# Unrolling attention's groups into one order, loading the first group during the projection, and moving the routing steps into attention

## The chip, the cores and the metric

The kernel runs on one core of a Trainium2 chip. Its time is the device time of one execution in microseconds (us). It was run three times: 2694.41, 2698.81 and 2700.54 us, with a median of 2698.81 us. The engines are named as in the profile: PE (TensorE), PEld (its weight loads), DVE (VectorE), ACT (ScalarE), POOL (GpSimd), and SP (SyncE), which only starts transfers here.

## What is computed

Two layers. Each one normalises its input, runs an attention and a routed feed-forward part on it, and adds the product of the two to the input. The change touches the first layer's attention and the routing of its feed-forward part:

```python
xn = _layernorm(x, axis=-1)                      # x: [2, 2048, 256]
# attention: 16 heads of 16 channels, causal, exact softmax
q, k, v = (xn @ W.T).reshape(B, S, 16, 16).transpose(0, 2, 1, 3)   # for Wq, Wk, Wv
p = softmax(where(mask, q @ k.T / 4, min)); out = (p @ v) @ Wo.T
# routing: 8 experts, each takes its first C = 4096/8 = 512 tokens
logits = x_flat @ router_w; probs = softmax(logits)
expert_idx = argmax(probs); gate = probs[expert_idx]
pos = cumsum(onehot)[expert_idx] - 1; keep = pos < C
expert_in.at[expert_idx, clip(pos, 0, C - 1)].add(x_flat * keep)
...
x = x + attention * silu(feed_forward)
```

## The kernel before, in words

The program is a row of stages, each a block that all engines enter and leave together: constants, projection (`stage_project`), attention (`stage_attention`), experts, a join, and the second layer. The change touches projection and attention.

**Projection.** 4096 tokens go through in 8 chunks of 512 (`NC`), four for each of the two sequences. For each chunk DVE normalises, PE turns the rows and multiplies them, and ACT and DVE together split each of q and k into three bf16 parts (`parts`, four tiles m = 0 to 3, each with parts 0, 1, 2). ACT makes the first part (`first`), DVE the rest (`rest_of`), ACT the second part, DVE the third. SP then stores them to `qk_parts` and v to `v`. `parts` is one buffer, so ACT's `first(m)` of a chunk waits until the store of the chunk before has landed (`parts_stored[m]`). POOL keeps a copy of the normalised rows (`xn_all`). After the last chunk DVE computes the routing from `logits` in 22 small steps (the first maximum, its one-hot form, counts through two matmuls of PE, the place of each token, the gate), with one exponential on ACT.

**Attention.** A group is four heads of one sequence; there are 8 groups (g), even ones of sequence 0, odd ones of sequence 1, and `u = g % 2` picks the buffers `qa`, `kb` (the parts of q and k, stacked to 96 rows) and `vg` (v with a column of ones). Each group needs three kinds of work:

- A steps: PE multiplies 128 queries by up to 512 keys into one of three `ring` banks, DVE takes the row maxima of it (`a_best`, line 859). There are 160 in a group: 16, 32, 48 and 64 for the query chunks c = 0 to 3.
- M and MT: after a chunk's last A step DVE negates the maxima and splits them in three (M), PE turns them and DVE copies them out (MT), and SP stores them as three further rows of `qa` (`store_rows`).
- S, PV, COPY, O: with those rows in place PE computes the scores again transposed (S, `a_pss`, line 774), ACT takes the exponential (line 836), PE multiplies by v (PV, `a_acc`, line 792), ACT copies the sums (COPY), PE turns them (O) and DVE divides.

An S step of chunk c waits for the chunk's three rows (`m_landed[c]`). `attention_steps` writes the order out by hand: a head of A steps up to half of group 0's cost (`LEAD = 0.5`), and then for each group a list in which its S and PV steps are woven with the second half of its own A steps and the first half of the next group's. Each group's list ends with its own last PV, COPY and O. All engines follow it in order: three times round a hardware loop over two groups (`groups`), then the last two groups written out. SP loads the next group (24 transfers of q, 6 of k, 4 of v) when a group begins. The first group is loaded after the projection has ended: q and v by SP (`load_q`, `load_v`), k by ACT.

POOL meanwhile sets `vg` and the ones in `kb`, writes zeros over `expert_in` (16 transfers) and then scatters the rows of `xn_all` to their experts' slots (32 indirect transfers).

Of the kernel before, what the change touches and what calls it, by code (L numbers as in the profile page):

```python
# [24 lines left out]
P = 128  # L25
# [194 lines left out]
def stage_project(nc, io, keep, dram):  # L220


    with ExitStack() as ctx:
# [14 lines left out]
        parts = st.sb("parts", [P, 4, 3, CH], BF16)  # L238
        vout = st.sb("vout", [P, 2, TC, D])
        spare = st.sb("spare", [P, 1])  # L240
        logits = st.sb("logits", [P, E, NT])
        top = st.sb("top", [P, NT])
        equal = st.sb("equal", [P, E, NT])
        first = st.sb("first", [P, NT])
        onehot = st.sb("onehot", [P, E, NT])
        onehot16 = st.sb("onehot16", [P, E, NT], BF16)
        shifted = st.sb("shifted", [P, E, NT])
        expd = st.sb("expd", [P, E, NT])
        total = st.sb("total", [P, E, NT])
        scanned = st.sb("scanned", [P, E, NT])  # L250
        place = st.sb("place", [P, E, NT])
        small = st.sb("small", [P, 6, NT])
# [12 lines left out]
        parts_stored = [st.sem(f"parts_stored{k}") for k in range(4)]  # L265
# [3 lines left out]
        onehot_ready, counted, shifted_ready, exp_ready = (st.sem("onehot_ready"), st.sem("counted"),  # L269
                                                           st.sem("shifted_ready"), st.sem("exp_ready"))  # L270
# [3 lines left out]
        @block.gpsimd  # L274
        def _(pool):
            def keep_copy(c, n, u):

                pool.wait_ge(xn_ready, c + 1)
                pool.tensor_copy(keep["xn_all"][:, bass.ds(c * TC, TC), :], xn[:, u, :, :]).then_inc(xn_kept, 1)

            chunks_skewed(pool, keep_copy, lambda c, n, u: None)

        @block.sync
        def _(sp):
# [18 lines left out]
            def store(c, u):  # L303
                at = snap(sp, c * CH)
                for m in range(4):
                    rows = dram["qk_parts"][m // 2, :, (m % 2) * P:(m % 2 + 1) * P, bass.ds(at, CH)]
                    sp.wait_ge(parts_ready, 4 * c + m + 1)
                    sp.dma_start(rows.rearrange("r p n -> p r n"), parts[:, m, :, :]).then_inc(parts_stored[m], 16)
# [13 lines left out]
            for m in range(4):  # L322
                sp.wait_ge(parts_stored[m], 16 * NC)
            for u in range(2):
                sp.wait_ge(v_stored[u], 16 * (NC // 2))

        @block.vector
        def _(vec):
# [34 lines left out]
            def back(c, n, u):  # L363
                def rest_of(m):

                    vec.wait_ge(first_part, 4 * c + m + 1)
                    vec.scalar_tensor_tensor(out=rest[:, m, :], in0=psq[m][:, :], scalar=HD ** -0.5 if m < 2 else 1.0,
                                             in1=parts[:, m, 0, :], op0=ALU.mult, op1=ALU.subtract).then_inc(rest_ready, 1)

                def third(m):  # L370
                    vec.wait_ge(second_part, 4 * c + m + 1)
                    vec.tensor_tensor(parts[:, m, 2, :], rest[:, m, :], parts[:, m, 1, :], ALU.subtract
# [4 lines left out]
                for m in range(4):  # L377
# [5 lines left out]
            ch.base, ch.k = NORM_STEPS * NC, 0  # L383


            vec.wait_ge(v_copied, NT)
            L = logits[:, :, :]
            first_max(vec, ch, keep, L, top[:, :], equal[:, :, :], first[:, :], onehot[:, :, :])
            vec.tensor_copy(onehot16[:, :, :], onehot[:, :, :]).then_inc(onehot_ready, 1)
            vec.tensor_tensor(shifted[:, :, :], L, top[:, :].unsqueeze(1).to_broadcast([P, E, NT]), ALU.subtract  # L390
                              ).then_inc(shifted_ready, 1)
            vec.wait_ge(exp_ready, 1)
            den, kept, chosen, clipped, slot = (small[:, k, :] for k in range(5))
            ch.link(vec.tensor_reduce(den, expd[:, :, :].rearrange("p e t -> p t e"), X, ALU.add))
            ch.link(vec.reciprocal(keep["gate"][:, :], den))
            vec.wait_ge(counted, 1)
            places(vec, ch, keep, "running0", psq[0][:, 0:E * NT], psq[1][:, 0:E * NT], total[:, :, :], scanned[:, :, :],
                   place[:, :, :])
            ch.link(vec.tensor_tensor(place[:, :, :], place[:, :, :], onehot[:, :, :], ALU.mult))
            ch.link(vec.tensor_reduce(chosen, place[:, :, :].rearrange("p e t -> p t e"), X, ALU.add))  # L400
            ch.link(vec.tensor_scalar(kept, chosen, float(CAP0), None, ALU.is_lt))
            ch.link(vec.tensor_tensor(keep["gate"][:, :], keep["gate"][:, :], kept, ALU.mult))
            ch.link(vec.tensor_scalar(clipped, chosen, float(CAP0 - 1), None, ALU.min))
            ch.link(vec.scalar_tensor_tensor(out=slot, in0=first[:, :], scalar=float(CAP0), in1=clipped,
                                             op0=ALU.mult, op1=ALU.add))
            ch.link(vec.tensor_copy(keep["slot_get"][:, :], slot))

            ch.link(vec.scalar_tensor_tensor(out=clipped, in0=kept, scalar=-SKIP, in1=slot, op0=ALU.mult, op1=ALU.add))
# [83 lines left out]

def attention_steps():

    maxima, ends = [], []
    for c in range(QC):
# [1497 lines left out]
```

## Time and profile before

| What | us |
|---|---|
| median of 3 runs | 2698.81 (2694.41 to 2700.54) |
| span of the profiled execution | 2692.8 |
| PE busy in the span | 2451.3 (91%) |
| DVE busy | 1846.2 (69%) |
| ACT busy | 1406.8 (52%) |
| POOL busy | 815.1 (30%) |
| v_rows<-p_vout, issue to landing, median | 5.1 |
| a_qa<-a_neg_rows in the attention, issue to landing: least, median, most | 1.6, 1.9, 3.5 |
| last transfer of attention issued by ACT | 1156.86 |

The span runs from the first to the last instruction of one profiled execution; the measured time also holds what lies before and after. The profiled execution's own measured time is not given apart; the median of the runs is 6.0 us above its span. The mean granted PE clock over the span is 0.953 of full speed. Times in rows are counted from the span's start, so an instruction's place in the table of stages can be read off directly: projection until about 133, attention from there to about 1159.

### The profile page before, as it was taken

The page shows a single profiled execution, that of the slowest core. Times are in us where ns is not written, and L with a number is a line of the kernel's source. Part 1 is how long each engine was busy: PE and PEld are TensorE (multiplying, and loading weights), DVE is VectorE, ACT ScalarE, POOL GpSimd, SP SyncE. Part 2 cuts the span into 40 slices and gives each one's busy share as a digit, 9 for nine tenths or more (in the row PEclk, how much of TensorE's full clock was granted, in tenths as well). Part 3 has the DMA queues.
Part 4 walks back from the last instruction along what each step waited for, and adds up shares of the span by engine and source line. Part 5 has one row for each costly group of instructions (what it writes and reads, how often), then busy time and mean ns, then how long its engine had stood idle before and what let it go on. Part 6 is the DMA issues. An engine that isn't in the chain of part 4 may idle for free. (4 is left out here: it accounts for less than half of the span.)

```text
span 2692.8 us, 51134 instructions
## 1 busy us (share of the span) xinstructions
PE 2451.3 (91%) x16420; PEld 1589.0 (59%) x16420; DVE 1846.2 (69%) x3682; ACT 1406.8 (52%) x2776; POOL 815.1 (30%) x647
## 2 busy tenths in 40 slices
PE   5648999999999999969977599999999999999999
PEld 4512333333333333358866477777777777777777
DVE  7757877877787777424438476777667767766776
ACT  3404655656565566755634255555555555555554
POOL 1070000000000000014425355554455555444553
PEclk9858999999999999989988699999999999999999
DMA  4574041321404040033257000000000000000000
GB/s 135 191 170 65 5 62 26 41 52 16 61 6 62 6 60 5 7 127 133 102 177 241 18 13 12 11 13 13 13 13 13 9 11 13 13 13 13 13 9 9
DMA packets 189865, 132.85 MB, mean 49 GB/s; under 512 B 99857, under 2 KB 177687, under 8 KB 189712
## 3 DMA queue, kind: packets, MB, share of 16 engines
q1 hardware_dynamic: 160048, 100.06, 15.4%
q10 hardware_dynamic: 24160, 14.16, 2.2%
q0 software_dynamic: 5504, 16.69, 1.7%
q8 instruction: 83, 1.36, 0.2%
q14 instruction: 70, 0.57, 0.1%
HBM read 84.43 MB, written 46.14 MB: 48 GB/s over the span
## 5 line engine op out<-in xcount | busy, mean ns | idle before, releaser
L859 DVE TENSOR_REDUCE a_best<-a_ring 128x1 f32<-128x512 f32 (+3 forms) x1280 | 700.9, 604 | 214.0 <-PE a_ring L721 123.0
L836 ACT ACTIVATE a_probs<-a_pss 128x1024 f32<-128x1024 f32 (+3 forms) x640 | 554.0, 895 | 452.6 <-PE a_pss L777 228.7
L721 PE MATMUL a_ring<-a_kb,a_qa 96*128 96x512 bf16 (+3 forms) x1280 | 453.0, 365 | 67.2 <-DVE a_best L859 32.3
L774 PE MATMUL a_pss<-a_qa,a_kb 99*128 99x512 bf16 (+3 forms) x1280 | 433.9, 353 | 15.6 <-issue 7.2
L1771 ACT ACTIVATE w_probs<-w_pss,w_top 128x256 f32<-128x256 f32 x512 | 239.0, 476 | 379.7 <-DVE w_top L1859 365.0
L1606 POOL TENSOR_TENSOR w_probs<-w_probs,w_inv 128x512 f32<-128x512 f32 x256 | 301.0, 1176 | 395.7 <-DVE w_inv L1865 386.3
L962 POOL TENSOR_TENSOR e_w_r<-e_w,e_w_r 128x1024 fp32r<-128x1024 f32 x28 | 67.0, 2402 | 1032.7 <-ACT e_w_r L1035 1032.7
L1629 PE MATMUL w_psw<-wqkv,w_xr 128*128 128x512 f32 x1152 | 301.5, 398 | 11.6 <-POOL w_xr L1563 11.6
L774 PEld LDWEIGHTS a_pss<-a_qa,a_kb 99*128 99x128 bf16 x1280 | 123.5, 98 | 302.6 <-ACT a_probs L836 224.5
L792 PE MATMUL a_acc<-a_probs,a_vg 128*32 128x512 f32 (+3 forms) x2560 | 299.9, 541 | 0.1
L1669 PE MATMUL w_pss<-w_kd,w_qt 128*128 128x256 f32 x1536 | 278.4, 310 | 0.0
L1859 DVE TENSOR_REDUCE w_top<-w_pss 128x2 f32<-128x512 f32 x256 | 176.8, 691 | 141.5 <-PE w_pss L1669 140.7
L721 PEld LDWEIGHTS a_ring<-a_kb,a_qa 96*128 96x128 bf16 x1280 | 126.4, 99 | 223.9 <-DVE a_best L859 128.6
L1629 PEld LDWEIGHTS w_psw<-wqkv,w_xr 128*128 128x128 f32 x1152 | 205.6, 190 | 47.6 <-POOL w_xr L1563 12.1
L1669 PEld LDWEIGHTS w_pss<-w_kd,w_qt 128*128 128x128 f32 x1536 | 222.0, 195 | 4.1
L1629 PE MATMUL w_psw<-we,w_xr 128*128 128x512 f32 x768 | 204.2, 401 | 0.0
L1710 PE MATMUL w_pso<-w_pt,w_v 128*64 128x128 f32 x2048 | 168.3, 285 | 0.1
L1689 PE MATMUL w_pst<-identity,w_probs 128*128 128x128 f32 x1024 | 155.7, 275 | 0.0
L1629 PEld LDWEIGHTS w_psw<-we,w_xr 128*128 128x128 f32 x768 | 134.9, 188 | 22.9 <-issue 0.2
L1689 PEld LDWEIGHTS w_pst<-identity,w_probs 128*128 128x128 f32 x1024 | 123.6, 140 | 31.2 <-issue 5.7
L1882 DVE SCALAR_TENSOR_TENSOR w_y<-w_psw,coef,w_y 128x256 f32<-128x256 f32 x224 | 108.3, 484 | 42.4 <-PE w_psw L1629 23.2
L1710 PEld LDWEIGHTS w_pso<-w_pt,w_v 128*64 128x64 f32 x2048 | 106.5, 136 | 49.6 <-issue 49.1
(223 smaller groups left out, 3771.2 us busy)
## 6 DMA issues: line engine op xcount, KB each, us to landing
e_w<-in_w SPq DMA_DIRECT2D x16, 1024.0 KB, 7.9
qk_parts<-p_parts SPq DMA_DIRECT2D x32, 384.0 KB, 3.7
a_qa<-qk_parts SPq DMA_DIRECT2D x192, 64.0 KB, 2.5
a_kb<-qk_parts SPq DMA_DIRECT2D x42, 256.0 KB, 9.5
p_xin<-in_x SPq DMA_DIRECT2D x8, 512.0 KB, 5.4
v_rows<-p_vout SPq DMA_DIRECT2D x8, 512.0 KB, 5.1
a_vg<-v_rows SPq DMA_DIRECT2D x32, 128.0 KB, 9.1
expert_in<-zero POOLq DMA_DIRECT2D x16, 256.0 KB, 8.3
```

Source lines behind the costliest of these rows:

```text
L721: ins = pe.matmul(bank[:, 0:keys], qa[u][0:QR, i // TC, h, (i % TC) * P:(i % TC + 1) * P], kb[u][0:QR, h, k * CH:k * CH + keys], start=Tru ...
L774: ins = pe.matmul(pss[idx % 2][:, e, lo:CH], kb[u][0:MR, h, j * P:(j + 1) * P], qa[u][0:MR, c, h, lo:CH], start=True, stop=(j < TC * c))
L792: ins = pe.matmul(acc[32 * h:32 * h + 32, lo:CH], vg[u][:, j, h, :], probs[:, 2 * (pv % 2) + h // 2, h % 2, lo:CH], start=(j == 0), stop=( ...
L836: act.activation(probs[:, idx % 4, :, lo:CH], pss[idx % 2][:, :, lo:CH], ACT.Exp).then_inc(exp_done, 1)
L859: vec.tensor_reduce(best[:, i // TC, h * TC + i % TC, k:k + 1], bank[:, 0:keys], X, ALU.max).then_inc(ring_taken, 1)
L1606: pool.tensor_tensor(probs[:, p % 4, :, :], probs[:, p % 4, :, :], inv[:, :, p:p + 1].to_broadcast([P, 2, 2 * P]), ALU.mult).then_inc(p_re ...
L1629: ins = pe.matmul(psw[bank][:, :], xr[a][:, src, k, :], moving(b, k), start=(m == 0), stop=(m == len(pairs) - 1))
L1669: ins = pe.matmul(scores, qt[a][:, p, :], keys[b][:, p, :, :], start=False, stop=(a, b) == PARTS[-1])
L1689: ins = pe.transpose(pst[r % 2][:, 2 * e + role, :], probs[:, p % 4, e, role * P:(role + 1) * P], keep["identity"][:, :])
L1710: ins = pe.matmul(pso[e * DH:(e + 1) * DH, p % 4, :], v[(u + 1 + role) % 2][:, h * DH:(h + 1) * DH], pt[:, p % 2, 2 * e + role, :], start= ...
L1771: ins = act.activation(probs[:, p % 4, e, :], pss[p % 2][:, e, :], ACT.Exp, bias=top[:, e, p:p + 1], accum_out=rows[:, e, p:p + 1])
L1859: vec.tensor_reduce(top[:, :, p], pss[p % 2][:, :, :], X, ALU.max, negate=True).then_inc(top_ready, 1)
```

## The change

There are four parts.

1. `attention_plan` replaces `attention_steps`. It makes one order for all 8 groups; no engine has a loop in the attention any more. A steps lead the S steps by 0.3 of a group at first (`LEAD0`), then grow at 1.3 times the rate of S (`RAISE`) up to a lead of 0.6 (`LEAD`). So the head has 53 A steps in place of 84, group 1's A steps begin at 0.54 of group 0's S work, and the last 0.6 of the last group has no A step. A group's last O now stands some steps into the next group.
2. The first group's q, k and v are loaded by POOL in the projection, after its copy of chunk 5 (`c == NC // B + 1`), once chunks 0 to 3 are stored. The buffers of even groups and `logits` live in `EarlyGroup`. POOL sets the ones and zeros in them when the projection starts.
3. `parts` has two buffers, one for each parity of the chunk.
4. The routing steps stand in the attention's order, one (`RT`) behind each of the first 22 A steps of group 2, that is from 1.40 to 1.51 groups of S work. The scatter waits for the last of them (`slots_ready`).

The core of the diff:

```diff
@@ projection, POOL
-            chunks_skewed(pool, keep_copy, lambda c, n, u: None)
+            ch.link(pool.memset(early.vg[:, :, :, :], 0.0))
+            ch.link(pool.memset(early.vg[:, :, :, HD:HD + 1], 1.0))
+            ch.link(pool.memset(early.kb[QR:MR, :, :], 1.0))
+            for c in range(NC):
                 pool.wait_ge(xn_ready, c + 1)
+                pool.tensor_copy(keep["xn_all"][:, c * TC:(c + 1) * TC, :], xn[:, c % 2, :, :]).then_inc(xn_kept, 1)
+                if c == NC // B + 1:
+
+                    for u in range(2):
+                        for m in range(4):
+                            pool.wait_ge(parts_stored[u][m], 16 * NC // B // 2)
+                        pool.wait_ge(v_stored[u], 16 * NC // B // 2)
+                    group_k(pool, dram, [early.kb], 0, early.k_landed)
+                    group_q(pool, dram, [early.qa], 0, early.q_landed)
+                    group_v(pool, dram, [early.vg], 0, early.v_landed)
@@ projection, ACT
-                    wait(act, parts_stored[m], 16 * c)
-                    act.activation(parts[:, m, 0, :], psq[m][:, :], ACT.Copy, scale=HD ** -0.5 if m < 2 else 1.0
+                    wait(act, parts_stored[u][m], 16 * n)
+                    act.activation(parts[:, u, m, 0, :], psq[m][:, :], ACT.Copy, scale=HD ** -0.5 if m < 2 else 1.0
@@ the order
-LEAD = 0.5
+LEAD0, LEAD, RAISE = 0.3, 0.6, 1.3
+ROUTE_STEPS = 22
+ROUTE_AT = 2
+    def wanted(done):
+
+        at = done / total
+        return LEAD0 + RAISE * at if RAISE * at + LEAD0 < at + LEAD else at + LEAD
+
+    def advance(done, turn_later):
+        nonlocal found, routed
+        while found < wanted(done) * whole:
+            u = next(ahead, None)
+            if u is None:
+                return
+            if u[0] == "MT" and turn_later:
+                late.append([u, 6])
+                continue
+            steps.append(u)
+            if u[0] == "A":
+                found += cost(u[2:])
+                if u[1] >= ROUTE_AT and routed < ROUTE_STEPS:
+                    steps.append(("RT", routed))
+                    routed += 1
@@ attention, SP
+            begun = -1
+            for s, r in plan:
+                if s[0] == "S" and s[1] > begun:
+                    begun = s[1]
+                    if begun + 1 < GROUPS:
+
+                        wait(sp, pv_done, begun * n_pv)
+                        load(begun + 1)
                 if s[0] == "MT":
-                    store_rows(0, s[2], r)
+                    assert s[1] <= begun + 1
+                    store_rows(s[1], s[2], r)
@@ attention, POOL
             pool.wait_ge(cleared, 16 * n)
+            pool.wait_ge(slots_ready, 1)
```

On POOL the order of instructions in the projection shows where the first group's transfers stand. `p_` names are the projection's, `g_` those of the early group, `a_` the attention's:

```order
-L274 UNCONDITIONAL_BRANCH
-L279 COPY xn_all<-p_xn 128x1024 x3
+L261 UNCONDITIONAL_BRANCH
+L264 MEMSET g_vg 128x2048
+L266 MEMSET g_vg 128x64
+L267 MEMSET g_kb 3x8192
+L270 COPY xn_all<-p_xn 128x1024 x6
+L562 DMA g_kb<-qk_parts 16x4x2048 x6
+L553 DMA g_qa<-qk_parts 16x4x512 x24
+L571 DMA g_vg<-v_rows 128x16x16 x4
+L270 COPY xn_all<-p_xn 128x1024 x2
```

The three sets and 34 transfers are new there; two copies of rows stand behind the transfers.

On PE, before, the end of the head and the first S step (line 774) stand behind the A steps (line 721, with its mask on line 724) of chunk 2, and behind a loop's entry:

```order
L721 MATMUL a_ring<-a_kb,a_qa 128x512 x2
L721 MATMUL a_ring<-a_kb,a_qa 128x384
L724 MATMUL a_ring<-mask_qk,identity 128x128
L721 MATMUL a_ring<-a_kb,a_qa 128x512 x3
L724 MATMUL a_ring<-mask_qk,identity 128x128
L632 UNCONDITIONAL_BRANCH
L632 ISA
L773 ISA
L774 MATMUL a_pss<-a_qa,a_kb 128x512
```

After, on PE, the same place: the turn of chunk 1's maxima (line 729), five A steps of chunk 2, and the first S step (line 755):

```order
L729 MATMUL a_ring<-identity,a_neg_parts 128x128
L702 MATMUL a_ring<-g_kb,g_qa 128x512 x2
L702 MATMUL a_ring<-g_kb,g_qa 128x128
L705 MATMUL a_ring<-mask_qk,identity 128x128
L702 MATMUL a_ring<-g_kb,g_qa 128x512 x2
L755 MATMUL a_pss<-g_qa,g_kb 128x512
L758 MATMUL a_pss<-mask_kq,identity 128x128
```

So 31 A steps of group 0 moved behind the first S step, and the branches are gone.

On DVE, after, the routing steps stand between the maxima (line 904) of group 2's first A steps:

```order
L904 TENSOR_REDUCE a_best<-a_ring 128x1
L845 TENSOR_REDUCE a_top<-g_logits 128x32
L904 TENSOR_REDUCE a_best<-a_ring 128x1
L847 TENSOR_TENSOR a_r_equal<-g_logits,a_top 128x256
L904 TENSOR_REDUCE a_best<-a_ring 128x1
L849 SCALAR_TENSOR_TENSOR a_r_equal<-a_r_equal,expert 128x256
L904 TENSOR_REDUCE a_best<-a_ring 128x1
L852 TENSOR_REDUCE a_first<-a_r_equal 128x32
```

Before, they stood behind the projection's last `p_parts` and ahead of everything in the attention.

## Rows read from the trace of the kernel before

**Rows 1.** Busy time of each engine by stage (windows); x is a count.

```profile
core 0: us, PE busy (x) PEld busy (x) DVE busy (x) ACT busy (x) POOL busy (x), PEclk, DMA share, GB/s
78.00:122.00 44.00, 34.23 (x195) 29.09 (x193) 32.86 (x89) 26.72 (x68) 2.09 (x2) 0.96 0.57 192
133.00:151.00 18.00, 0.00 (x0) 0.00 (x0) 0.00 (x0) 0.00 (x0) 17.77 (x7) 0.50 1.01 126
183.00:215.00 32.00, 6.73 (x17) 1.30 (x16) 6.71 (x12) 0.00 (x0) 21.01 (x22) 0.50 0.30 111
...
340.60:458.70 118.10, 113.08 (x788) 43.23 (x788) 93.33 (x192) 71.09 (x85) 0.00 (x0) 1.00 0.25 37
...
1058.80:1160.00 101.20, 94.32 (x662) 32.46 (x662) 48.51 (x98) 70.37 (x85) 0.00 (x0) 1.00 0.04 8
```

**Rows 2.** Timeline at the projection's end: start, us, engine, line [idle before <-releaser].

```profile
113.03 0.60 ACT L425 ACTIVATE p_parts<-p_psq 128x512 bf16<-128x512 f32 x1 [1.93 <-DMA qk_parts<-p_parts]
122.88 0.58 DVE L144 TENSOR_REDUCE p_top<-p_logits 128x32 f32<-128x256 f32 x1
123.97 1.10 SPq L310 DMA_DIRECT2D v_rows<-p_vout  x1
132.09 0.18 DVE L409 TENSOR_SCALAR slot_put<-p_small 128x32 uint32<-128x32 f32 x1
```

**Rows 3.** Timeline of the first group's load and the first A step.

```profile
144.22 24.40 SPq L683 DMA_DIRECT2D a_vg<-v_rows  x4
151.23 0.29 PE L721 MATMUL a_ring<-a_kb,a_qa 96*128 96x128 bf16 x1 [24.79 <-DMA a_kb<-qk_parts]
```

**Rows 4.** Timeline of the head, up to the first S step.

```profile
161.28 16.03 DVE L859 TENSOR_REDUCE a_best<-a_ring 128x1 f32<-128x512 f32 x32 [0.21 <-PE a_ring L721]
178.86 0.22 DVE L876 COPY a_neg_rows<-a_ring 48x128 bf16<-48x128 bf16 x1 [0.38 <-PE a_ring L731]
182.57 38.85 SPq L641 DMA_DIRECT2D a_qa<-qk_parts  x24
203.69 0.29 DVE L859 TENSOR_REDUCE a_best<-a_ring 128x1 f32<-128x128 f32 x1 [4.90 <-remote]
223.60 0.63 PE L774 MATMUL a_pss<-a_qa,a_kb 99*128 99x512 bf16 x1
```

**Rows 5.** Waits in 223:1160: who waited for whom, us, times, longest.

```profile
PE a_pss L774 <- issue: 7.2, 2, 3.6
PE a_ring L802 <- ACT a_sums L844: 6.1, 8, 0.8
PE a_pss L774 <- DMA a_qa<-a_neg_rows: 5.8, 4, 1.6
```

**Rows 6.** Issue of transfers on SP and POOL: timeline, and the tile expert_in.

```profile
72.57 1.05 POOL L279 COPY xn_all<-p_xn 128x1024 f32 x1 [10.70 <-DVE p_xn L216]
75.68 2.75 SPq L308 DMA_DIRECT2D qk_parts<-p_parts  x4
...
L668 POOL DMA_INDIRECT expert_in<-xn_all,slot_put x32: 977/982/1042, 169.5 to 209.4; - x32
L665 POOL DMA_DIRECT2D expert_in<-zero x16: 539/542/771, 150.8 to 159.0; - x16
...
355.21 14.25 SPq L683 DMA_DIRECT2D a_vg<-v_rows  x4
1205.90 0.84 POOL L986 DMA_DIRECT2D expert_out<-e_yout  x1 [5.19 <-DVE e_yout L1093]
```

**Rows 7.** Timeline rows in which POOL and DVE use SBUF.

```profile
12.27 0.17 DVE L212 COPY p_var<-p_mv 128x4 f32<-128x4 f32 x1
16.30 1.43 POOL L279 COPY xn_all<-p_xn 128x1024 f32<-128x1024 f32 x1 [10.54 <-DVE p_xn L216]
137.02 13.79 POOL L660 MEMSET a_kb<- 3x8192 bf16 x2
```

**Rows 8.** Timeline of ACT near the attention's end.

```profile
1145.93 4.02 ACT L836 ACTIVATE a_probs<-a_pss 128x1024 f32<-128x1024 f32 x4 [0.26 <-PE a_pss L774]
```

More of the change, by code:

```diff
@@ L382, in _ @@
             chunks_skewed(vec, front, back)
[L383 to L408, printed above, removed]
-            ch.link(vec.tensor_scalar(keep["slot_put"][:, :], clipped, SKIP, None, ALU.add))
         @block.scalar
@@ L519, in attention_steps @@
     whole = sum(cost(u) for u in maxima)
-    lead, at = 0, 0
-    while at < LEAD * whole:
-        at += cost(maxima[lead])
-        lead += 1
-    def flow(lo, hi, dg):
-        for n in range(lo, hi):
-            yield ("A", dg, *maxima[n])
+    pairs = [(g, c, j) for g in range(GROUPS) for c in range(QC) for j in range(TC * (c + 1))]
+    total = sum(width(c, j) for g, c, j in pairs if g == 0) * GH
+    ahead = []
+    for g in range(GROUPS):
+        for n, u in enumerate(maxima):
+            ahead.append(("A", g, *u))
@@ L568, in attention_steps @@
[L568 to L588 removed]
+                ahead += [("M", g, c), ("MT", g, c)]
@@ new lines, in attention_plan @@
+    ahead = iter(ahead)
+    steps, late, found, routed = [], [], 0, 0
+    def wanted(done):
[16 more added lines that the diff above has]
+                    routed += 1
@@ new lines, in attention_plan @@
+    done = 0
+    advance(0, False)
+    for n, (g, c, j) in enumerate(pairs):
+        for h in range(GH):
+            steps.append(("S", g, c, j, h))
+            done += width(c, j)
+            advance(done, True)
+            for item in late:
+                item[1] -= 1
+            while late and late[0][1] <= 0:
+                steps.append(late.pop(0)[0])
+        if n:
+            pg, pc, pj = pairs[n - 1]
+            steps.append(("PV", pg, pc, pj))
+            if pj == TC * (pc + 1) - 1:
+                steps.append(("COPY", pg, pc))
+                late.append([("O", pg, pc), 6])
@@ L849, in _ @@
+            store(*turned_at[1:])
         @block.vector
@@ L872, in take_rows @@
-            def take_rows(c, r, bank, landed):
-                vec.wait_ge(ring_full, r + 1)
-                wait(vec, m_landed[(c - 2) % QC], landed)
-                vec.tensor_copy(neg_rows[:, c % 2, :], bank[0:3 * GH * TC, 0:P // 2].bitcast(BF16)).then_inc(ring_taken, 1)
+            L, (equal, onehot, shifted, expd, scanned, place) = logits[:, :, :], (big[n][:, :, :] for n in big)
+            before, total = counts[:, 0, :, :], counts[:, 1, :, :]
+            den, kept, chosen, clipped, slot = (small[:, k, :] for k in range(5))
```

565 lines of the change are left out of this document (281 added, 284 removed).

## The prediction, made before the changed kernel was run

> **What bounds the kernel now.** I read the table of stages first, then the timeline across the two stages that change, then the waits of the attention. The stages show two kinds of time [rows 1]. In the stream of the attention PE bounds: in the whole group from 340.6 to 458.7 PE is busy 113.1 of 118.1 us, DVE 93.3, ACT 71.1. Work that moves into this stream costs PE time; work that leaves other engines there costs nothing. Ahead of the stream nearly nothing is bound by PE: from 133 to 151 PE and DVE do nothing at all, and from 183 to 215 both work under 7 of 32 us.
>
> The timeline gives the reasons. The projection ends with 9.4 us of routing on DVE, 122.88 to 132.27 [rows 2]. Then the first group is loaded, and PE's first A step at 151.23 has waited 24.8 us for `a_kb` [rows 3]. The head runs at DVE's pace, 32 maxima in 16.03 us, and has finished chunks 0 and 1 at 179.1; then it stalls: at 203.69 DVE takes a tile that PE multiplied about 10 us before. That stretch begins when SP starts the next group's q transfers (182.57; 24 of them take 38.85 us) while POOL's scatter runs (169.5 to 209.4), and ends soon after the scatter. The first S step is at 223.60 [rows 4]. In the stream the chain of waits holds little: 7.2 us in two places where PE goes round the loop, 6.1 us before the O of each group, 5.8 us for the maxima's rows at chunk 3 [rows 5].
>
> **The sum, part by part.** It is made against the profiled execution (span 2692.8; the median is 6.0 us above it, and I carry this over).
>
> *Start of the attention.* Routing leaves the end of the projection, but the block can't end before the last v store has landed: issued at 123.97, with the 5 us that such a store takes, 129 [rows 2]. The second `parts` buffer draws that in. In the middle of the projection DVE bounds and nothing is gained. In the last two chunks, which have no normalisation beside them, ACT waits for the stores before (1.93 us at 113.03, about as much a chunk earlier, and DVE and PE wait behind it [rows 2]): 4.6 us. So the store lands at 124.3, and the next stage's first instruction follows 0.6 us later, as now. For contention and for the start (below) I add 2.4 us, between 0 and 9: first A step at 127.3, not 151.2. **-23.9 us.**
>
> This rests on the load being hidden. POOL is free after its copy of chunk 5 (72.57), chunk 3 is stored about 83.3 (its stores begin at 75.68, and v's comes last) [rows 6]. The 30 transfers of q and k have 64 rows each; the zeros' transfers, 128 rows, take 0.54 us: 16.2 us. v's 4 transfers have 2048 pieces of 64 bytes. No row shows such a transfer on POOL: below it lies 0.54, above it the scatter's pace, 1.29 us for 128 rows, or 20.6 us. `expert_out` (512 rows, 0.84 us) in proportion gives 3.4, and SP takes 3.6 for the same transfer [rows 6]; I take 3.4. POOL is then done at 83.3 + 16.2 + 13.6 = 113.1, with its last two copies at 115.2, 9 us before the store lands. If each v transfer took over 5.6 us, the stage would end later by the surplus. The bytes fit: the DMA queues are at 0.57 from 78 to 122 [rows 1].
>
> One new cost is at the start. POOL now sets `g_kb` from about 8.3 for 6.9 us, while DVE's first small copies start at 12.27 [rows 7]. If the two exclude each other, the projection starts up to 3.0 us later. They can get in each other's way: POOL's copy of rows takes 1.43 us at 16.30 beside a DVE cast, and 1.05 later [rows 6, 7]. This trace agrees there with the Trainium skill, SBUF — State Buffer, section Who interferes with whom: an operation of DVE in its two-port modes and one of GpSimd hold a shared port for the whole instruction.
>
> *Head.* Now 72.4 us, 151.2 to 223.6. Chunks 0 and 1 stay (27.6 us [rows 3, 4]), then 5 A steps instead of 36 at 0.5 to 0.55 us: 30.4 us. The stall between 183 and 215 has no place here: SP's load of group 1 starts when S begins, and the scatter has moved away from it. **-42.0 us.** First S step at 157.7.
>
> *Stream, now 223.6 to 1157.3.* Two trips round the loop go: **-7.2**. Seven of eight group ends no longer drain before O (0.78 us each): **-5.5**. The wait for the maxima's rows goes in steady groups, where M of chunk 3 now leads by 0.17 of a group, -5.8 and a little more that PEld shows; but in group 0 the lead is thin. Chunk 2's maxima turn 2.5 full-width S steps ahead of need and chunk 3's 1.5, or 2.4 and 1.4 us, against 6 us from turn to landing: about +8 for both, the first just behind SP's v transfers. Together **+0.3**, with -6 and +6 as bounds.
>
> The 31 A steps that left the head are now PE's work. The last group, with 76 A steps in place of 160, lasts 98.5 us where a whole one lasts 118.4 [rows 1]: 0.26 us per step missing, with little of the wide ones' difference in it, so **+8.1**. Routing costs 9.4 us of DVE [rows 2] at 1.40 to 1.51 of the stream, a stretch of 12 us. There the A steps are of chunk 0, short for PE, and DVE alone needs about 12 us for them and their M. PE is only three banks ahead, so little of it hides: between 0 and 9.4, I take **+7**. From 0 to 1.0 the A steps run at 1.3 times the pace; DVE (93.3 x 1.3 = 121 us) then comes close to PE's 130: **+3** (0 to 8). In the last 0.6 group there are no A steps; full-width exponentials go back to back at 1.005 us [rows 8], 2.0 a pair of tiles against PE's 1.92, for some 20 pairs: **+2** (0 to 4).
>
> Sum: -23.9 - 42.0 - 7.2 - 5.5 + 0.3 + 8.1 + 7 + 3 + 2 = **-58.2 us**, 2698.8 - 58.2 = 2640.6, said as 2641. The experts' stage and all behind it shift as they are.
>
> **Rivals.**
>
> *A, slower: POOL's descriptors are slow.* If POOL's transfers follow the scatter's row, 1.29 us each for q and k and 20.6 for v [rows 6], POOL ends at 83.3 + 38.7 + 82.4 + 2.1 = 206.5, first A step 207.3, 80 us later than in the sum: 2721. It decides from 14.5 us per v transfer on. For it: 2048 pieces are more than any POOL row here has. Against: `expert_out` costs 1.6 ns per row. Chance 0.04.
>
> *B: the stall comes back.* Its cause isn't shown by the trace, only its company, scatter beside q transfers. If the scatter alone against the full stream is enough, or group 1's load at the head's end, the lost share of 183 to 215, 0.79 [rows 1], applies to at most the scatter's 41 us: +32, or 2673. Against: from 169.5 to 179 the scatter ran and DVE took its maxima back to back [rows 4], and loads in later groups cost nothing visible. In the new order the scatter runs from about 1.5 to 1.86, between group 2's load (to 1.25) and group 3's (2.0). Chance 0.12.
>
> *C: POOL issues only where DVE lets it.* DVE is busy 32.9 of 44 us at the place [rows 1]. If POOL gets only the gaps, 9 of its 30 us are done when DVE ends near 118, and the rest ends at 139: first A step at 142, 15 us later, 2655. Against: the scatter's time, 0.98, is the same beside a busy and an idle DVE (977 to 1042 ns, all 32) [rows 6]. The Trainium skill, SBUF — State Buffer, section SBUF: two separate sides, speaks against this change: a DMA issued from GpSimd is starved of descriptors while DVE is in such a mode. By its figures (about 620 ns alone, 3100 beside such copies) 34 transfers would be an estimated 105 us and the gain nearly gone. Behind that sentence stands what the same page says of reductions, that they don't contend; the trace agrees, with those 0.98 us beside maxima, and shows no transfer of POOL beside the projection's copies. Chance 0.07.
>
> **How the numbers follow.** The forecast's case has 0.74; its own range is 2624 to 2661, from the bounds taken together with some luck on both sides. Something else, such as PE waiting in the new order where I see nothing, has 0.03. The range of 2622 to 2668 leaves out A, the upper half of B and the tails. A measurement of this kernel tells about 0.2% (5 us) from no change. Faster by more: 0.94; within 0.2%: 0.02; slower: 0.04.
>
> **What the changed profile should show.** POOL's transfers of `g_vg` done before 116, and no wait of PE for `g_kb`; first A step near 127; first S step near 158, with no "remote" waits of DVE before it; no 3.6 us holes in the stream; a wait of 3 to 5 us for `a_neg_rows` at group 0's chunks 2 and 3, and none later; about 7 us of PE waiting for DVE at the routing; ACT bound at the end. The prediction is wrong if POOL still issues after 124, if PE and DVE slow during the scatter, or if a steady group takes other than 116 to 118 us.

## The result, and the profile after

The changed kernel takes 2683.63 us (median of 4 runs, 2679.45 to 2685.58), the kernel before 2699.68 (4 runs, 2694.41 to 2705.18). The ratio is 0.9932, with a 95% interval of 0.991 to 0.9954: faster, but by 16 us, where 58 were forecast. The time lies above the range.

The last v store, the first A step, the first S step and the experts' first load, from the timelines of the changed kernel (start us, us, engine, line; they answer to [rows 2 to 4]):

```profile
138.91 1.10 SPq L308 DMA_DIRECT2D v_rows<-p_vout  x1
144.37 0.27 PE L702 MATMUL a_ring<-g_kb,g_qa 96*128 96x128 bf16 x1 [9.98 <-PEq L223]
174.34 0.63 PE L755 MATMUL a_pss<-g_qa,g_kb 99*128 99x512 bf16 x1
1148.07 0.39 SPq L993 DMA_DIRECT2D e_rows<-expert_in  x1
```

The A steps begin 6.9 us earlier than before, not 23.9; the head is 30.0 us long, as forecast; and from the first S step to the experts it takes 973.7 us where before takes 935.7. Two places account for it. The first is the projection, while POOL loads the first group. Here are POOL's and SP's transfers in the changed kernel's timeline, and the waits from 90 to 125 (who waited, for what: us, times, longest):

```profile
88.12 3.30 POOL L562 DMA_DIRECT2D g_kb<-qk_parts  x6 [10.79 <-DMA v_rows<-p_vout]
91.40 12.29 POOL L553 DMA_DIRECT2D g_qa<-qk_parts  x24
103.67 4.65 POOL L571 DMA_DIRECT2D g_vg<-v_rows  x4
108.29 2.06 POOL L270 COPY xn_all<-p_xn 128x1024 f32<-128x1024 f32 x2
```

```profile
95.19 8.75 SPq L308 DMA_DIRECT2D v_rows<-p_vout  x1
103.98 14.14 SPq L306 DMA_DIRECT2D qk_parts<-p_parts  x4
```

```profile
ACT p_parts L397 <- DMA qk_parts<-p_parts: 13.5, 4, 4.5
DVE p_rest L366 <- ACT p_parts L397: 12.0, 4, 4.4
PE p_psv L427 <- ACT g_logits L409: 11.7, 1, 11.7
```

POOL is done at 110.4, earlier than I had worked out. But SP's one v store now takes 8.75 us to issue where it took 1.1, four stores of parts take 14.14 where they took 2.75, ACT waits 13.5 us for stores to land, and PE stands still for 11.7. The windows (as [rows 1]) say why, and show the second place, group 1:

```profile
90.00:100.00 10.00, 7.95 (x46) 6.76 (x45) 9.48 (x34) 6.12 (x16) 10.00 (x20) 1.00 1.07 127
100.00:110.00 10.00, 9.65 (x44) 8.15 (x44) 6.55 (x11) 3.98 (x7) 10.00 (x14) 0.83 1.02 213
110.00:120.00 10.00, 0.00 (x0) 0.00 (x0) 1.49 (x3) 1.79 (x3) 0.35 (x1) 0.69 1.06 244
378.00:392.00 14.00, 7.26 (x58) 3.06 (x56) 3.89 (x9) 3.29 (x5) 10.79 (x11) 0.82 0.24 96
392.00:406.00 14.00, 1.67 (x13) 0.55 (x12) 0.69 (x1) 0.60 (x1) 10.80 (x11) 0.50 0.25 103
406.00:420.00 14.00, 2.08 (x6) 0.69 (x6) 0.69 (x1) 0.38 (x1) 9.83 (x11) 0.50 0.24 97
475.10:591.10 116.00, 112.44 (x790) 43.19 (x790) 93.43 (x194) 72.01 (x86) 0.00 (x0) 1.00 0.26 38
1085.00:1145.00 60.00, 57.94 (x397) 16.66 (x395) 12.33 (x29) 49.13 (x58) 0.00 (x0) 1.00 0.03 6
```

The last column but one is the share of the DMA queues: full from 90 to 120. From 378 to 420 POOL issues the scatter (377.9 to 418.9), the queues are at 0.25, and PE, DVE and ACT do almost nothing. That is the picture of 183 to 215 before [rows 1], with no q transfer of SP in it. The waits of group 1, 314 to 475, in the changed kernel:

```profile
ACT a_probs L816 <- remote: 37.4, 4, 20.5
DVE a_best L904 <- remote: 34.7, 3, 16.2
PE a_pss L755 <- issue: 27.8, 3, 19.3
```

"remote" and "issue" mean that the profile shows no instruction or transfer of this core whose end released the waiting engine. In the trace's semaphore events (the signals between engines) it is PE's own signals that come late, that of a matmul done at 391.8 at 409.3 for one, while DVE and PE move on within about 0.1 us of an end on the other engines: DVE's signal follows its maximum at 393.1 at once, and PE starts at 393.76 behind an exponential of ACT that ended at 393.71. The ends of matmuls are modelled in a profile, so a signal that came late and a matmul that itself ended late look the same here. Group 1 takes 161.3 us (SP's loads at 313.84 and 475.13), the groups from 2 to 5 take 115.9 each.

### The profile page after: what moved, and what is told of

The parts are those of the page before. It is cut to its first block and busy times, and to the rows that moved or that the text cites. A ratio compares the mean times of both kernels' runs of the same rounds, so it can differ in the third digit from the quotient of the medians.

```text
span 2682.1 us, 47620 instructions
## 1 busy us (share of the span) xinstructions
PE 2448.7 (91%) x16420; PEld 1588.8 (59%) x16420; DVE 1850.1 (69%) x3682; ACT 1414.8 (53%) x2776; POOL 836.8 (31%) x681
## 5 line engine op out<-in xcount | busy, mean ns | idle before, releaser
L816 ACT ACTIVATE a_probs<-a_pss 128x1024 f32<-128x1024 f32 (+3 forms) x640 | 560.9, 896 | 431.0 <-PE a_pss L755 221.1
L702 PE MATMUL a_ring<-g_kb,g_qa 96*128 96x512 bf16 (+3 forms) x640 | 228.1, 370 | 26.7 <-DVE a_best L904 13.9
L755 PE MATMUL a_pss<-a_qa,a_kb 99*128 99x512 bf16 (+3 forms) x640 | 212.9, 353 | 34.9 <-issue 27.8
L702 PE MATMUL a_ring<-a_kb,a_qa 96*128 96x512 bf16 (+3 forms) x640 | 218.3, 350 | 14.7 <-DVE a_best L904 11.5
L755 PE MATMUL a_pss<-g_qa,g_kb 99*128 99x512 bf16 (+3 forms) x640 | 219.9, 352 | 1.4 <-DMA g_qa<-a_neg_rows 0.8
L755 PEld LDWEIGHTS a_pss<-a_qa,a_kb 99*128 99x128 bf16 x640 | 60.2, 98 | 180.2 <-ACT a_probs L816 110.1
L777 PE MATMUL a_acc<-a_probs,a_vg 128*32 128x512 f32 (+3 forms) x1280 | 151.5, 546 | 0.0
L777 PE MATMUL a_acc<-a_probs,g_vg 128*32 128x512 f32 (+3 forms) x1280 | 150.0, 541 | 0.0
L755 PEld LDWEIGHTS a_pss<-g_qa,g_kb 99*128 99x128 bf16 x640 | 62.3, 98 | 139.3 <-ACT a_probs L816 99.1
```

What stands on the lines that cost most here:

```text
L702: ins = pe.matmul(bank[:, 0:keys], qa[u][0:QR, i // TC, h, (i % TC) * P:(i % TC + 1) * P], kb[u][0:QR, h, k * CH:k * CH + keys], start=Tru ...
L755: ins = pe.matmul(pss[idx % 2][:, e, lo:CH], kb[u][0:MR, h, j * P:(j + 1) * P], qa[u][0:MR, c, h, lo:CH], start=True, stop=(j < TC * c))
L777: ins = pe.matmul(acc[32 * h:32 * h + 32, lo:CH], vg[u][:, j, h, :], probs[:, 2 * (pv % 2) + h // 2, h % 2, lo:CH], start=(j == 0), stop=( ...
L816: act.activation(probs[:, idx % 4, :, lo:CH], pss[idx % 2][:, :, lo:CH], ACT.Exp).then_inc(exp_done, 1)
```

## Experiments

The experiments were run in six later series, on four different chips (which one the first runs had is not recorded), and there **both** kernels are faster: before takes 2664 to 2676, and the changed kernel 2641 to 2648. No trace of them shows the stall. That is why each run is set against its own series here. Names with a_ are the changed kernel with one thing altered, b_ is the kernel before with one thing altered, best2 and best3 are the changed kernel with several costs mended; each is described below. The table has every run: the time (median), the start of the first A step and of the first S step, the length of group 1 (from one load of SP to the next), and the experts' first load.

| kernel | time | A | S | group 1 | experts |
|---|---|---|---|---|---|
| before, first runs | 2699.7 | 151.2 | 223.6 | | 1159.3 |
| changed, first runs | 2683.6 | 144.4 | 174.3 | 161.3 | 1148.1 |
| before_again | 2664.6 (series 2671.7) | 152.0 | 197.9 | | 1131.7 |
| b_noscatter | 2668.5 (2672.1) | 152.2 | 198.1 | | 1131.6 |
| after_again | 2646.1 | 143.2 | 173.1 | 122.8 | 1108.7 |
| after_third | 2647.7 | 142.6 | 172.5 | 122.9 | 1108.5 |
| a_noscatter | 2643.4 | 140.0 | 170.0 | 123.3 | 1106.4 |
| a_direct, a_direct2 | 2643.2, 2646.3 | 142.7, 142.2 | 172.5, 172.1 | 124.8, 124.0 | 1109.8, 1108.7 |
| a_allate | 2646.3 | 146.9 | 176.5 | 122.9 | 1112.4 |
| a_vlate | 2641.0 | 136.9 | 166.8 | 122.8 | 1101.8 |
| a_paced | 2643.4 | 139.9 | 169.8 | 123.5 | 1106.5 |
| a_onesfirst | 2646.6 | 142.4 | 172.3 | 124.9 | 1109.8 |
| a_shortones | 2640.8 | 139.1 | 168.8 | 123.0 | 1104.4 |
| best2, best2_direct | 2644.6, 2645.6 | 135.4, 134.4 | 172.0, 170.9 | 122.8, 122.7 | 1107.4, 1106.3 |
| best3, best3_again | 2629.1, 2631.0 | 128.6, 128.4 | 158.2, 158.1 | 122.8, 122.9 | 1093.7, 1093.2 |
| best3_direct, best3_direct2 | 2628.6, 2632.9 | 128.0, 128.0 | 157.6, 157.6 | 122.7, 122.7 | 1092.7, 1093.4 |

Two spreads have to be kept in mind in reading it. Seven traces (the changed kernel's three, `a_noscatter`, `a_direct`, `a_direct2`, and, but for two sets in another order, `a_onesfirst`) do the same work up to the first A step, and it comes at 140.0 to 144.4. And behind the experts' first load every profiled execution takes another 1531 to 1538 us, whatever was changed ahead of it. So a difference of 3 us in one first A step, or of 5 in one time, proves nothing by itself. The head and the stream are steadier: without the stall they take 29.7 to 30.0 and 935.0 to 937.5 us in the changed order, `best2` and `best2_direct` apart.

**The scatter.** `a_noscatter` and `b_noscatter` delete POOL's loop over `indirect_dma_start` and the wait behind it; `a_direct` changes its transfers:

```diff
-                pool.indirect_dma_start(dram["expert_in"], bass.IndirectOffsetOnAxis(ap=keep["slot_put"][:, t:t + 1], axis=0),
...
+                pool.dma_start(dram["expert_in"][t * P:(t + 1) * P, :], keep["xn_all"][:, t, :]).then_inc(scattered, 16)
```

> The changed kernel with POOL's 32 scatter transfers of the routed rows left out (the experts then compute on zeros, the same number of instructions; all else is as in the changed kernel). Theory 1, the scatter holds PE up in group 1: group 1 shrinks from 161.3 us to the 116 of the others plus some 4 to 5 for the routing, so the whole is 38 to 42 us shorter, about 2643. Theory 2, the long group 1 comes of something else that lies there (the routing steps, group 2's load, the supply of PE's instructions in the unrolled order): group 1 stays near 160 us and the time near 2683.

> The changed kernel with each of the 32 scatter transfers replaced by a direct POOL transfer of the same 128 rows to consecutive rows of expert_in (the experts then get tokens in the order of the sequence, in place of the routed ones). If it is the gathering and scattering of descriptors made by GpSimd from indices that holds PE up, the stall is gone: about 2643. If any transfers that POOL issues, 4 MB in 32 pieces, do it, the stall is there again, shortened at most as the issue is (0.54 us in place of 1.29 each, so some 17 us of it): about 2660. If it is the written bytes alone, the same 2660 or a little more.

> The kernel before with its 32 scatter transfers left out (the experts then compute on zeros). Theory 1, the stall from 183 to 215 is the scatter's: 32 us at a share of 0.21 become about 7 us, so 24 to 27 us less than the kernel before, about 2673. Rival: it is the 24 q transfers of group 1 that SP issues there (38.85 us), with which the stall began: no change by leaving the scatter out, about 2699, and SP's 24 transfers still take about 39 us.

2643.4 and 2643.2 are the numbers that I had written for "the scatter does it", and they show nothing of the kind: in this series there was no stall to remove. The sign was `b_noscatter`, at 2668.5 within 4 us of the kernel before with its scatter. So I ran both kernels as they are.

> The changed kernel as it is, again, on a chip drawn anew. In the four runs of the last series the kernel before took 2672 where it had taken 2694 to 2705, and the one kernel of them that kept the scatter in the changed order showed no stall. Theory, the stall under the scatter belongs to some chips (or to some executions) and not to others, in both kernels alike: on a chip without it group 1 takes 123 us, the first A step comes at 142 to 145, and the whole is about 2645 beside 2672; with it 161 us and 2684 beside 2699. Rival, the stall belongs to the changed kernel's own order and moving v away from POOL had taken it away: 161 us and 2684 on any chip.

> The kernel before as it is, with a profile, beside the runs of this series. If the stall between 183 and 215 is what makes the difference between 2699 and 2672, then a run near 2672 shows the first S step near 198 and SP's 24 q transfers in 11 to 13 us, and a run near 2699 shows them as in the first trace (223.6, and 38.9 us).

The ratio is 0.9903 (0.9886 to 0.992). The kernel before, without the stall (PE's first S step, SP's q transfers of group 1; in the first runs: [rows 4]):

```profile
197.91 0.63 PE L774 MATMUL a_pss<-a_qa,a_kb 99*128 99x512 bf16 x1
181.94 11.56 SPq L641 DMA_DIRECT2D a_qa<-qk_parts  x24
```

And the changed kernel in group 1 under its scatter (376.99 to 417.9, the same pace), with its waits from 313 to 436:

```profile
378.00:392.00 14.00, 13.87 (x116) 6.02 (x109) 10.42 (x21) 8.55 (x13) 10.65 (x12) 1.00 0.27 105
392.00:406.00 14.00, 12.30 (x77) 4.10 (x76) 11.37 (x26) 7.57 (x8) 10.65 (x12) 1.00 0.32 115
406.00:420.00 14.00, 13.98 (x89) 4.53 (x86) 11.99 (x23) 9.63 (x10) 9.19 (x10) 1.00 0.22 88
```

```profile
PEld a_pss L755 <- ACT a_probs L816: 24.8, 30, 1.3
DVE a_best L904 <- PE a_ring L702: 12.8, 20, 0.9
```

No "remote" is left. The stall is worth 26.4 us of head before (72.4 against 45.9) and 38.1 in the stream of the changed kernel (973.7 against 935.6). The scatter alone isn't enough for it: on the later chips group 1 is as long with it (122.8) as without (123.3). Nor is it in the scatter's packets: the 4 KB ones in those 42 us took 158 ns in the first runs and 159 here.

Two further series put the kernel with the scatter beside the one with direct transfers, so that a chip with the stall would tell indices from bytes.

> The changed kernel with direct transfers of the same rows in place of the scatter (tokens in order in place of the routed ones), beside the one as it is. If that one stalls here: group 1 takes 123 us if the indirect form is what holds PE's signals up, 150 to 161 if any write of that size does. If it does not stall, the two are within 3 us of each other, as on the chip of the first series.

> The same with direct transfers of the same rows in place of the scatter (tokens in order in place of the routed ones). Without the stall within 3 us of the kernel with the scatter. With it: group 1 takes 123 us if the indirect form holds PE's signals up, 150 to 161 if any write of that size does.

> The changed kernel as it is, once more, to find a chip with the stall. With it: group 1 takes 161 us and the whole 2684, before 2699. Without it: 123 us, 2646 and 2671, as on the last chips.

Neither chip had it (`best3_again` stood beside the last), nor had those of two earlier series:

> The mended kernel with its 32 scatter transfers replaced by direct ones of the same rows to consecutive rows (tokens in order in place of the routed ones). On a chip without the stall it is within 3 us of the mended kernel. On a chip with it, this tells the indices from the bytes: if the indirect transfers hold PE's signals up, group 1 takes 123 us here and 161 in the mended kernel; if any write of that size does, both show it.

> The same with its 32 scatter transfers replaced by direct ones of the same rows to consecutive rows (tokens in order in place of the routed ones). On a chip without the stall within 3 us of the kernel with the scatter. On one with it: group 1 takes 123 us here and 161 there if the indirect form holds PE's signals up, both 161 if any write of that size does.

In all of them the direct form and the scatter are within 3 us of each other. Whether the scatter causes the stall or only coincides with it twice stays open. So does what brings it: all eight executions of the first runs are about as slow as the two that were profiled with the stall, and none of the later ones is, which speaks for the chip or its state at the time more than for chance in single executions, but the stall was never seen again to test it.

**The early load.** `a_vlate` moves one call from POOL in the projection to SP's start in the attention. `a_allate` moves all three there and leaves out POOL's waits for the stores.

```diff
-                    group_v(pool, dram, [early.vg], 0, early.v_landed)
...
+            group_v(sp, dram, vg, 0, early.v_landed)
```

> The changed kernel with only the four v transfers of group 0 (8192 pieces of 64 bytes) moved from POOL in the projection to SP at the attention's start, where the head's 30 us hide them. Theory by pieces, the v transfers fill the DMA queues from 100 to 120: the projection's last stores are issued 10 to 14 us earlier (from 136 to some 124), the first A step from 144.4 to about 132, and the whole about 2671. Theory by bytes (v is 0.5 MB of the 3.5 MB that POOL loads): 2 to 3 us less, about 2681. The stall in group 1 is as in the changed kernel in both.

> The changed kernel with no load in the projection: SP loads q, k and v of group 0 at the attention's start, as the kernel before does. If POOL's load (k and q, 3 MB, v, 0.5 MB in pieces) is what makes the projection's stores late, the projection ends at about the predicted 124 to 125 (last v store landed) plus 3 for the lock at the start, so its first wait begins near 128, and the first A step follows 17 to 18 us later (the load as in the kernel before): 145 to 146, so that the early load is worth no more than 1 to 3 us as it stands in the changed kernel, and some 9 with v late. Rival, POOL's load has nothing to do with it and the double buffer or the order does: the first A step near 162.

With all of it late the first A step comes at 146.9, the projection's last v store is issued at 124.07, and no v store of SP takes more than 1.11 us to issue. With all of it early, 143.2 in the same series: the early load as written is worth 3.7 us (2.5 to 6.9 by the spread above), and it makes the last v store 13.6 us later (137.67). With v alone late, 136.9, between the two theories. The packets of the trace give the sizes. In `a_allate` k is 384 packets of 4 KB at 514 ns each, 12.3 us of all sixteen DMA engines, and a store's packet of 1 KB takes some 50 ns. By POOL, k and q together are 768 packets of 4 KB, 19.2 us of all sixteen engines (in `best2`, below), and from 88 to 122 only 0.43 of 34 us, 15, were free. Both theories on v counted it wrongly: POOL's four v transfers went in 128 packets of 4 KB, some 2.9 us of all engines, and not in 8192 pieces of 64 bytes; SP's in later groups did go in 8192.

> The changed kernel with POOL's load in three parts (k and q of chunk 0 after the copy of chunk 5, q of chunks 1 to 3 after that of chunk 6, v after that of chunk 7), the memset where it was. If pace is what counts, it does as well as moving v away, or better: first A step between 131 and 137, about 2635 to 2641. If v's 8192 pieces cost the queues wherever they stand, they now meet the last stores: first A step at 140 to 143, 2643 to 2646.

With v kept and all of it spread, 139.9: no better than the earliest of the unchanged ones (140.0), so no gain is shown for pacing, and it did less than moving v (136.9). `best2` combined three things: v late, q in two parts, and the memset of the ones (6.9 us on POOL) moved behind the projection, into the attention:

> The changed kernel with three of its costs mended: POOL's load of q and k in two parts (k and q of chunk 0 after its copy of chunk 5, q of chunks 1 to 3 after its copy of chunk 6), v of group 0 by SP at the attention's start, and the 6.9 us memset of the ones moved behind the projection. If the full DMA queues are what makes the projection end late, and the rest of it is the lock, the last v store is issued near 122 and the first A step comes near 127 to 129, 14 to 16 us earlier than in the changed kernel and 8 to 10 earlier than with v late alone: about 2631 beside 2646 and 2672 on a chip without the stall, 2668 to 2670 beside 2684 and 2699 on one with it. Rival, the queues are full in shorter bursts all the same, because stores and loads together need the same time: the first A step near 134, about 2638.

The first A step came at 135.4, so the rival was right on the queues: POOL's copy of chunk 6 was due at once, and the second part of the load followed the first after 1.1 us. And the gain went again in the head, 36.5 us long instead of 30.0. Its timeline from 144, DVE and POOL:

```profile
144.29 7.00 DVE L916 CAST a_neg_parts<-a_neg_rest 128x16 bf16<-128x16 f32 x1
```

```profile
144.34 6.92 POOL L648 MEMSET a_kb<- 3x8192 bf16 x1
```

**The memset.** A cast of 16 numbers a row takes 7.00 us, and ends with POOL's memset. The changed kernel has the same at its start, on a copy of four numbers a row, which takes 0.17 us before [rows 7] (both rows from its first trace; DVE's, then POOL's):

```profile
12.10 3.24 DVE L212 COPY p_var<-p_mv 128x4 f32<-128x4 f32 x1
```

```profile
8.39 6.92 POOL L267 MEMSET g_kb<- 3x8192 bf16 x1
```

`a_onesfirst` only puts the long memset ahead of the two of `g_vg`. `a_shortones` writes the ones in pairs, 4096 values of four bytes in place of 8192 of two (here, and in the attention's own set-up):

```diff
-            ch.link(pool.memset(early.kb[QR:MR, :, :], 1.0))
+            ch.link(pool.memset(early.kb[QR:MR, :, :].bitcast(F32), TWO_ONES))
```

> The changed kernel with POOL's 6.9 us memset of the ones in g_kb ahead of the two of g_vg instead of behind them. Theory, DVE's small copy (3.24 us in place of 0.17, and its end is the memset's end, 15.3) waits for a shared SBUF port: the memset then ends at 13.2, the copy starts at 12.1 and takes about 1.1, and the projection and everything behind it comes 2.1 us earlier. Rival, the memset's total length matters, whatever the order: no change.

> The changed kernel with the ones written as pairs, nothing else changed. Theory, DVE's copy waits for the port that POOL's memset holds to its end: with the memset over at 11.9 the copy takes 0.17 us again, POOL's first copy starts near 16.3 (not 19.3), and all of the projection comes 3 us earlier; the first A step near 140. Rival, what the memset holds up is something else: no change before the first A step.

Swapped, the copy takes 1.08 us, but DVE's next instruction takes 1.82, as long as the memset of `g_vg` that now comes behind: POOL's first copy of rows starts at 18.86 instead of 19.27, 0.4 us gained, not 2.1. Halved, the memset ends at 11.9:

```profile
12.09 0.17 DVE L212 COPY p_var<-p_mv 128x4 f32<-128x4 f32 x1
```

```profile
8.37 3.51 POOL L267 MEMSET g_kb<- 3x4096 f32 x1
```

POOL's first copy starts at 16.21, 3.1 us earlier. The first A step comes at 139.1, which fits but is only 0.9 us outside the spread.

**What fits.** `best3` takes the short memset, and loads early only what the queues can take: k and one chunk of q by POOL, the rest by SP at the attention's start.

```diff
                     group_k(pool, dram, [early.kb], 0, early.k_landed)
-                    group_q(pool, dram, [early.qa], 0, early.q_landed)
-                    group_v(pool, dram, [early.vg], 0, early.v_landed)
+                    group_q(pool, dram, [early.qa], 0, early.q_landed, (0,))
...
+            group_q(sp, dram, qa, 0, early.q_landed, (1, 2, 3))
+            group_v(sp, dram, vg, 0, early.v_landed)
```

> The changed kernel with only k and q of chunk 0 loaded early by POOL, q of chunks 1 to 3 and v by SP at the attention's start, and the ones written as pairs (4096 values of four bytes with the bits of two ones, in place of 8192 of two). Theory, the projection's lateness is the time that the load takes on the DMA queues: k's 384 packets of 4 KB at some 510 ns each are 12.3 us of all sixteen engines, and q's 24 transfers 9 to 12 more, against 0.43 of 37 us that are free; k and one chunk of q fit, all of q does not. The memset now ends at 11.9, ahead of DVE's copy at 12.1. Then the last v store is issued near 121 and the first A step comes at 126 to 129, some 15 us earlier than in the changed kernel: 2630 to 2633 on a chip without the stall, 2667 to 2670 with it. Rival, k alone fills the queues against the stores of its moment and the order never recovers: first A at 134 and 2638.

> The kernel with k and one chunk of q early, and the short memset, again on a chip drawn anew. Without the stall 2627 to 2632 beside 2671, a ratio of 0.985 as in its first series. With the stall: group 1 takes 161 us, some 2667 beside 2699, a ratio of 0.988.

2629.07 beside 2670.23 (ratio 0.985, 0.9828 to 0.9871) and on another chip 2630.96 beside 2668.41 (0.9849, 0.9828 to 0.9871); the changed kernel's ratio on such chips is 0.9903. In its timeline (PE's first A and S step) and its windows:

```profile
128.57 0.27 PE L704 MATMUL a_ring<-g_kb,g_qa 96*128 96x128 bf16 x1 [9.99 <-PEq L223]
158.23 0.63 PE L757 MATMUL a_pss<-g_qa,g_kb 99*128 99x512 bf16 x1
```

```profile
90.00:100.00 10.00, 7.94 (x45) 7.02 (x45) 9.47 (x35) 5.62 (x15) 3.72 (x6) 0.88 1.03 124
100.00:110.00 10.00, 8.56 (x46) 7.24 (x46) 5.83 (x10) 4.72 (x13) 0.00 (x0) 0.94 1.07 351
110.00:120.00 10.00, 8.58 (x48) 7.26 (x47) 5.47 (x9) 7.42 (x21) 0.00 (x0) 1.00 0.87 298
```

POOL's load is now 480 packets of 4 KB, 14.3 us of all engines, against the 15 that were free. The queues are still full for 20 us, but PE works 8.58 of the 10 us in which it did nothing, and both steps stand within 1.3 us of where I had forecast them for the changed kernel (127.3, 157.7).

## Why the prediction was wrong

| part of the sum | forecast | first runs | later, without the stall |
|---|---|---|---|
| start, to the first A | -23.9 | -6.9 | -8.8 |
| head | -42.0 | -42.4 | -16.0 |
| stream, to the experts | +7.7 | +38.0 | +1.8 |
| median | -58.2 | -16.1 | -25.5 |

The last column sets `after_again` against `before_again`, its median against the series. The parts are read from one profile of each kernel, the medians from all runs, so they don't add up exactly: the parts of the first runs give -11.3, the spans of the two profiles differ by 10.7 and the medians by 16.1, since the first profile of before is that of a run at the short end of its four (span 2692.8). In the last column the parts give -23.0, the spans -17.5 and the medians -25.5.

*Start: mis-sized by 17 us, and the step is "The bytes fit: the DMA queues are at 0.57 from 78 to 122".* I compared bytes with a share of time. The row beside it says what this load costs: from 133 to 151 it holds the queues at 1.01 at only 126 GB/s [rows 1], 18 us of full queues, and by its packets that is k and less than half of q. 0.43 of the 34 us from 88 to 122 is 15. The term for contention and lock was 2.4 with a bound of 9; it measured 14 for the queues and 3.1 for the lock, against the 3.0 that I had as its most. Both are shown, by `a_allate` and `best3` and by `a_shortones`. The other 2 to 3 us of the 17 are stores that the projection issues later than I had worked out even without load and lock, and the spread of single traces. What isn't shown is how the 14 come about in full: POOL's packets take 22.8 us of all engines where 15 were free, a shortfall of 8; the rest may lie in the order in which stores, loads and ACT's waits follow each other, which no run takes apart. The rest of the step held: POOL was done before 116, no PE wait for `g_kb`, and the projection without the load issues its last v store at 124.07, or 121 less the lock, where I had 119. A v transfer took POOL 1.16 us, where I had put 3.4 from rows of other transfers; that error went the other way and cost nothing.

*Head: the number right, half its reason not.* 30.0 us for 30.4, with no stall in it. But "the scatter has moved away from it" was counted as a gain of the whole stall. In the first runs the stall moved with it.

*Stream: rival B.* The mechanism, the stall coming back under the scatter alone in group 1, is what that trace shows; I gave it 0.12 and 32 us, and it took 38 (group 1 at 161.3 where it takes 122.8 without). Its cause stays open; what failed is that I put its return at nothing in the sum. "From 169.5 to 179 the scatter ran and DVE took its maxima back to back" had spoken against it: 10 us without a stall at the scatter's start. The changed trace begins its scatter with some 4 such us too. What I should have asked is whether the stall belongs to the scatter or to the place. The remaining forecast was 6 us too high. Routing fits: group 1 without the stall is 122.8 where the steady ones are 115.9, 6.9 more for my +7, though no run moves the routing alone. The maxima's rows in group 0 cost 1.9 us at PE's loads, not 8, and at the end ACT doesn't bound: from 1085 to 1145 PE is busy 57.9 of 60 and ACT 49.1. Steady groups are 115.9, just under my 116 to 118.

*Rivals A and C* fell: POOL issued its 34 transfers in 20.2 us, 0.51 us each for q and 1.16 for v, with DVE busy 9.48 of 10 us beside it. The estimate of 105 us that I had worked out from the Trainium skill (SBUF — State Buffer, SBUF: two separate sides) did not come true. The rule itself is hardly put to the test, though: only 2.1 of those 20.2 us of DVE are copies and tensor-scalars, and the one q transfer that falls beside the longest of them (from 98.48) took 0.66 us instead of 0.51. My error was to count the whole of the projection's DVE work as such copies.

So the chances were wrong where two things that I held apart went wrong together: B and a start worth 7 instead of 24. That the later runs of the changed kernel, at 2646, lie in the range is no merit of it: before is 28 us lower there too.

## What to carry to other kernels

Budget a moved transfer in time of the DMA queues, not in bytes: read the share that it takes where it stands now, and set that against the free share of the place where it goes; load early only what fits, the rest where something hides it. When a stall's cause isn't known, don't book its going as a gain with the work that moves; ask whether it goes along, and run both unchanged kernels in the same series as any experiment on it, since one that removes nothing can still hit the expected number. A memset on few partitions takes as long as its elements a row want (6.92 us for 3 x 8192, 3.51 for 3 x 4096, 1.80 for 128 x 2048), and beside it a copy or a cast on DVE can stand as long: write it in wider elements, or put it where DVE only reduces.

## What the runs showed of the hardware

- A stall in the first profiles of both kernels and in none of the 18 later ones: by the trace PE's signals come 5 to over 20 us late (matmuls done at 391.8 and 392.1, signals at 409.3 and 414.2), while the signals of DVE and the scatter's packets (158 ns against 159) keep their pace. It cost 26 us before and 38 in the changed kernel.
- POOL's memset of 3 partitions by 8192 elements (6.92 us) holds a DVE copy, cast or tensor-scalar for the rest of its time (3.24, 7.00, and 1.82 beside a shorter one), but not a reduction out of PSUM: fourteen of them ran at their pace beside it in `best2` (280 to 692 ns, as before). The Trainium skill, SBUF — State Buffer, section Who interferes with whom, has this for DVE's two-port modes, and the trace agrees.
- Packets of one size took different times on a DMA engine: 4 KB of k 514 ns in the mean (`a_allate`), 4 KB of the q that POOL loads some 280 to 330 (`best2`), 4 KB of the scatter 158; a store's packet of 1 KB took some 50. By transfer k moves 8 bytes a ns and engine, a store some 20. What sets the time, the few partitions that k goes to or something else, no run separates.
- The engine that issues a load changes its packets: from the same expression POOL's q went in packets of 4 KB and SP's in packets of 1 KB, POOL's v in 4 KB and SP's in 64 bytes.
